# Audio tower on one core: the scan's input moves from PSUM to SBUF

## The reference, cut to what matters

```
def _ssm_layer(x, A_log, Dp, W_dbc, W_dt, b_dt):
    A = -jnp.exp(A_log)
    dbc = jnp.einsum('ble,ce->blc', x, W_dbc)
    delta, Bm, Cm = jnp.split(dbc, [DT_RANK, DT_RANK + N_STATE], axis=-1)
    delta = jax.nn.softplus(jnp.einsum('blr,er->ble', delta, W_dt) + b_dt)
    dA = jnp.exp(delta[..., None] * A)
    dBx = (delta * x)[..., None] * Bm[:, :, None, :]
    _, hs = jax.lax.associative_scan(combine, (dA, dBx), axis=1)   # h = dA * h_before + dBx
    y = jnp.einsum('blen,bln->ble', hs, Cm)
    return y + Dp * x
for i in range(NUM_LAYERS):            # 3 layers
    x = _ssm_layer(x, ...)
    if i < NUM_LAYERS - 1: x = mean of neighbouring pairs in time
h = _L0_tok_ref(x, ...)
h = h + _L0_attn_ref(_layernorm(h), ...)
h = h + _L0_ffn_ref(_layernorm(h), ...)
```

## Time and profile before

| | us |
|---|---|
| median of 3 runs | 638.44 |
| the profiled execution's own time | 639.52 |
| its span, first to last instruction | 637.8 |
| TensorE busy (matmul) | 568.4 (89%) |
| VectorE busy | 523.7 (82%) |
| ScalarE busy | 513.2 (80%) |
| GpSimd busy | 436.8 (68%) |

### The profile page before, as it was taken

One profiled execution on the slowest core, in us unless ns is written; L12 is line 12 of the kernel. 1 busy time (PEld: TensorE's weight loads), 2 busy tenths in 40 slices (PEclk: granted clock), 3 DMA queues, 4 the chain that ended last, 5 costly groups with the idle time before them and its releaser, 6 DMA issues.

```text
span 637.8 us, 22844 instructions
## 1 busy us (share of the span) xinstructions
PE 568.4 (89%) x9531; PEld 299.1 (47%) x9531; DVE 523.7 (82%) x924; ACT 513.2 (80%) x1044; POOL 436.8 (68%) x597
## 2 busy tenths in 40 slices
PE   3777678899999999999899999999999999999993
PEld 2333234545454554555454455554555544545441
DVE  5898999999979898988888988989799887653442
ACT  1335658989989999998888998999989887988780
POOL 7757899788777877876776777697785866423120
PEclk9999869999999999999999999999999999999996
DMA  3432223122121322122121222121200100000001
GB/s 78 84 80 65 57 56 73 43 59 54 40 51 26 79 50 49 36 55 52 24 61 42 61 48 60 41 65 36 65 21 20 28 20 15 20 15 10 7 13 30
DMA packets 77574, 28.51 MB, mean 45 GB/s; under 512 B 69271, under 2 KB 77463, under 8 KB 77463
## 3 DMA queue, kind: packets, MB, share of 16 engines
q1 hardware_dynamic: 71290, 25.92, 17.9%
q10 hardware_dynamic: 6173, 1.05, 0.9%
HBM read 13.25 MB, written 3.05 MB: 26 GB/s over the span
## 4 chain that ended last, share of the span: by engine, by line
PE 55%; DVE 16%; ACT 14%; POOL 6%; issue 4%; ACTq 2%; DMA 1%; SPq 1%; DVEq 0%; POOLq 0%
PE ring L1283 8%; PE ring L1362 6%; PE ring L1375 6%; PE ring L1470 5%; PE ring L1269 4%; PE ring L1441 3%; PE ring L1450 3%; PE ring L1258 2%; ACT pm L1066 2%; DVE ring L1732 2%; PE ring L1238 2%; PE ring L1421 2%; PE ring L1352 2%; DVE hidw L1860 2%; ACT hid L1116 1%
## 5 line engine op out<-in xcount | busy, mean ns | idle before, releaser
L1066 ACT ACTIVATE pm<-ring 93x744 f32<-93x744 f32 x128 | 96.3, 782 | 11.0 <-PE ring L1362 10.0
L1362 PE MATMUL ring<-q_exp,qk 32*93 32x372 f32 x512 | 56.2, 507 | 7.7 <-POOL q_exp L910 1.1
L1860 DVE TENSOR_TENSOR hidw<-hid,ring 128x744 f32<-128x744 f32 x48 | 44.3, 923 | 17.9 <-PE ring L1431 13.3
L1375 PE MATMUL ring<-pm,v 97*32 97x93 f32 x2048 | 53.5, 245 | 1.3 <-DVE base_A L1736 0.6
L1109 ACT ACTIVATE hid<-ring,b_col 128x372 f32<-128x372 f32 x96 | 49.4, 568 | 4.1 <-PE ring L1450 3.0
L1375 PEld LDWEIGHTS ring<-pm,v 97*32 97x32 f32 x2048 | 41.7, 109 | 16.0 <-ACT pm L1066 3.4
L910 POOL TENSOR_TENSOR q_exp<-qk,mask_q 128x1488 f32<-128x1488 f32 x16 | 43.0, 2687 | 8.9 <-DVE qk L1790 8.9
L1116 ACT ACTIVATE hid<-ring,b_col 128x744 f32<-128x744 f32 x48 | 42.2, 879 | 7.6 <-PE ring L1441 5.7
L893 POOL TENSOR_TENSOR base_C<-base_C,carry_C 128x744 f32<-128x744 f32 x16 | 28.4, 1777 | 27.1 <-DVE carry_C L1741 19.1
L1441 PE MATMUL ring<-hid,w 64*64 64x372 f32 x384 | 40.1, 488 | 0.6 <-ACT rows_hi_D L990 0.3
L1450 PE MATMUL ring<-nrm_f,w 64*64 64x372 f32 x384 | 39.4, 485 | 0.0
(11 more groups left out here) (366 smaller groups left out, 1757.2 us busy)
## 6 DMA issues: line engine op xcount, KB each, us to landing
xin_A<-in_x_dram SPq DMA_DIRECT2D x62, 93.0 KB
xin_B<-in_x_dram SPq DMA_DIRECT2D x62, 93.0 KB
x_A<-x_A SPq DMA_DIRECT2D x32, 93.0 KB, 3.0
x_B<-x_B SPq DMA_DIRECT2D x32, 93.0 KB, 2.7
x_C<-x_C SPq DMA_DIRECT2D x32, 93.0 KB, 2.2
out_dram<-osb SPq DMA_DIRECT2D x15, 186.0 KB
x_D<-x_D SPq DMA_DIRECT2D x32, 46.5 KB, 2.3
w<-in_L_ffn_expert_w_dram SPq DMA_DIRECT2D x6, 48.0 KB
```

What stands on the lines that cost most here:

```text
L1066: a.activation(pm[q % 2][h][0:TOUT].rearrange("m a j n -> m a (j n)"), out_of(f"att.s{q}{h}", g)[0:TOUT, :, 0:COLS], ACT.Square, bias=2.0, ...
L1362: ins = mm(o[h][0:TOUT, b, 0:COLS], qk[r:r + 32, 1, q * TOUT:(q + 1) * TOUT], q_exp[r:r + 32, q].rearrange("p j n -> p (j n)"), start=True ...
L1375: ins = mm(o[32 * j:32 * j + 32, 0, h * TOUT:h * TOUT + TOUT], rows[:, at:at + 32], pm[q % 2][h][:, b, j, :], start=(b == 0), stop=(b == 1 ...
L1860: tt(hidw[k][:], hid2[:], out_of(f"ffn.g_{k}", g)[:, :, 0:COLS], ALU.mult).then_inc(me, 1)
```

## The change

The step `vin` writes its product into the SBUF tile `carry` instead of its own PSUM banks, and the scan reads and writes that tile in place. So the wait for the `y` of the group before moves from `scan` to `vin`, and the banks of job `b` are free as soon as `vin` has ended.

```
-                for j, r in (("z", "quad"), ("b", "scan"), ("s", "based"), ("c", "carry"))}
+                for j, r in (("z", "quad"), ("b", "vin"), ("s", "based"), ("c", "carry"))}
...
                 if s == "vin":
                     need(g, f"pe {u}.b")
                     need(g, f"pool {u}.du")
-                    tt(b_made(u, g), b_made(u, g), du[u][:], ALU.mult).then_inc(me, 1)
+                    need(g, f"pool {u}.y", back=1)
+                    tt(carry[u][:], b_made(u, g), du[u][:], ALU.mult).then_inc(me, 1)
                 if s == "scan":
                     need(g, f"dve {u}.vin", f"act {u}.decay")
-                    need(g, f"pool {u}.y", back=1)
-                    v.tensor_tensor_scan(carry[u][:], dec[u][:], b_made(u, g), 0.0, ALU.mult, ALU.add).then_inc(me, 1)
+                    v.tensor_tensor_scan(carry[u][:], dec[u][:], carry[u][:], 0.0, ALU.mult, ALU.add).then_inc(me, 1)
```

The five strings of `ORDER` are new throughout. The same steps stand in them, 1000 on TensorE before and now, in another order and with other banks. A line of TensorE's and one of VectorE's:

```
-                    "att.s2:5/6,2! att.rs:6/0 ffn.h2_2:3/4! ffn.rs:4/6! att.qk:6/0 A.c:8/2! ffn.rh:4/6 B.z:9/4! B.b:9/6! "
+                    "A.c:8/2! ffn.rh:4/6 B.z:9/4! D.row:7/1! att.y2:5/2! B.b:9/6! att.s1:5/4,0! ffn.lg:4/3 ffn.g_2:3/0! "
...
-                    "A.carry:8 B.quad:9 B.vin:9 B.scan:9 ffn.route1:4 ffn.hidw2:3 B.most:9 ffn.top:4 ffn.fin:3 D.quad:7 att.hs:6 "
+                    "ffn.hn:4 A.carry:8 B.quad:9 B.vin:9 ffn.route1:4 ffn.hidw2:3 att.hs:6 ffn.top:4 A.most:9 B.scan:9 ffn.fin:3 "
```

## The result

The changed kernel takes 694.70 us (median of 3 runs, 693.01 to 695.31) against 638.44 us; the ratio is 1.0857, 95% interval 1.0832 to 1.0883. I had forecast 662.5 us, with a range of 641 to 692. The way was right, the size was not: it lost 56 us where I had forecast 24.

What follows compares the result with a forecast made beforehand. Three nearly full engines in a static order (TensorE 96%, ScalarE 92%, VectorE 89%) were taken to leave little room; 639.5 - 1.5 - 6 + 20 + 11 = 663.0, predicted as 662.5 us, range 641 to 692.

Steps and rivals of the forecast that it cites:

- Durations: In vin and the scans: vin 927 ns against 935, each scan some 18 ns shorter; 1.5 us less for both together.
- Banks freed earlier: At TensorE's waits that ended with a scan: vin frees the banks of b earlier, -6 us, bounds 0 and -12.6.
- VectorE stands still: At the scans, now with two SBUF inputs: VectorE waits for GpSimd instructions, 34 to 48 us, taken as 40.
- GpSimd is held: Where GpSimd's next instruction falls in a scan, it waits for the scan's rest: 44 us with the present positions.
- The rows of `rest` and the rests: Rows of a small two-SBUF-input VectorE instruction: it stands until GpSimd's is over, 0.14 us covered, losing 2 of 5 gapless boundaries.
- How much of this reaches the end: Over the whole kernel: half of VectorE's delay, 20 us, and a quarter of GpSimd's, 11 us, lengthen the run.
- Rival 1: At the scans: they don't take GpSimd's port, so only earlier banks and durations count; 631 us, chance 0.12.
- rival 2: At the scans: stalls come but fall into VectorE's and GpSimd's idle time; 642.5 us, chance 0.11.
- Rival 3: At gapless GpSimd boundaries: scans lose more often than 2 in 5, VectorE becomes the bound; 701 us, chance 0.07.
- Some 92%: TensorE's busy share from 120 to 500 us, forecast to fall from 96% to about 92%.
- The scans' means of 2.2 to 2.4 us: Sign in the changed profile: groups of scans would have a mean of 2.2 to 2.4 us, well over 1700 ns.
- TensorE's clock: In the steady stretch: the granted clock was expected to stay full; under full would add an uncounted cost.

Runs made afterwards that it cites:

- e2: The changed kernel with its orders and banks, each scan replaced by a reduction of the same length reading one SBUF tensor, recurrence left out: 633.7 us, ratio 0.9899.
- e3: The kernel before with old orders and the new step, each scan replaced by a same-length reduction reading one SBUF tensor: 639.9 us, ratio 1.0012.
- e1: The kernel before with its own orders and banks, only the step changed (vin writes the carry tile, scan works there): 695.2 us, ratio 1.0885.
- e10: As e6, with each VectorE stall half as long (31 of them, 18.2 us): 649.2 us, ratio 1.0137.
- e6: e2 with the changed kernel's 43 VectorE stalls (37.8 us) put back as idle reductions ahead of the scans: 669.9 us, ratio 1.0462.
- e7: e2 with the changed kernel's 51 GpSimd stalls (57.4 us) put back as idle additions: 664.0 us, ratio 1.0373.

## Why the prediction was right in its direction and wrong in its size

- *Durations.* `vin` 927 ns as forecast. A scan that nothing holds takes 1689 to 1708 ns, 1678 to 1704 before: the 18 ns that I took off each don't show. Together some 0.5 us, where I had 1.5.
- *Banks freed earlier,* -6 us: e2 has 0.9899 of before, 6.4 us, but that my number meets it is in part luck. I had it from the waits that ended with a scan (half of 12.6 us), and with the old order the earlier release gave nothing (e3). Only with the new order does it bring something, and I had not told the two apart.
- *VectorE stands still,* 34 to 48 us, I took 40: measured 37.8. *GpSimd is held,* 44 us: measured 57.4, so I was too small by 13. That is worth 3 us at my share. The new order is not why: with the old one (e1) GpSimd's busy time rose by 58.9 us, from 436.8 to 495.7. I had read it off the positions of the kernel before. 31 of the 51 holds were of 1.27 to 1.41 us: a scan that gets in where one GpSimd instruction ends meets the next one at its start and holds it for nearly the whole scan, which the old positions don't show.
- *The rows of `rest` and the rests.* Of VectorE's 34 us for the instructions under way, the trace gives 31 when 0.14 us are taken off each, as I said I did; that is worth under 2 us. And where I wrote that `rest` at 524.32 us starts before a GpSimd addition, it starts inside another GpSimd instruction (the row below, which I had left out). So it was passed over at three gapless boundaries there, 3 of 6 and not 2 of 5. The scans' 9 of 29 came out lower than either.

```profile
524.12 0.33 POOL L919 TENSOR_SCALAR oh<-logit 93x48 f32<-93x48 f32 x1
```

- *How much of this reaches the end.* Here the prediction failed. "I let half of VectorE's delay through: 20 us", and a quarter of GpSimd's, 11 us: 31 us. Measured, 62.7 us reached the end. VectorE's share alone is 96 to 97% (e10, e6), GpSimd's alone 59% (e7), both together 66%. With 66% of my own 40 + 44 the sum would have been 639.5 - 7.5 + 55 = 687, 686 in the median's terms. (The sum as I had it gives 661.9 in those terms; I wrote 662.5.)

Why the shares were wrong: I read 40 us of VectorE's idle time as room for delays. It isn't. With 37 us of work put ahead of the scans (e6), VectorE was busy 380.0 of 420 us, 90%, and 377.7 in e2; over the whole run it was idle for 110.6 us in e6 and 110.7 in e2, so its idle time did not shrink. TensorE's busy time in the 420 us fell instead, from 405 to 385. The waits of that stretch say how: those of TensorE's weight loads that ended with VectorE sum to 46 us in e2 and 68 in e6, and ScalarE's that ended with TensorE to 26 and 55. The longest of those of TensorE that ended with VectorE in e6 (us in total, times, longest) stands behind the 5.40 us of work put ahead of one scan of unit C:

```profile
PEld ring L1397 <- DVE attT L1808: 5.6, 1, 5.6
```

A delay of one engine turns into a wait of the others a few jobs on. The chain of waits had hinted at it: it changes engine all the time. From it I took the engine's share of the chain (19%) as a lower end, and that said little about VectorE: the chain shows one path, and others through VectorE must have been nearly as long, which no view shows directly; in e6 VectorE has 29% of the chain, 17% in e2.

Rival 1 (scans don't take the port) and rival 2 (idle time takes the stalls in) are out. Rival 3 (VectorE starves) named a mechanism that is there, 9 passed boundaries and stalls of 4.5 and 5.4 us, but it is not what made the size: VectorE stood for 37.8 us, within my bounds. "Some 92%" for TensorE was wrong: 88%. The scans' means of 2.2 to 2.4 us, which I had named as a sign, hold for A and C alone; B's is 1.88, and D's 1.90 where 0.92 is its own length. TensorE's clock, which I took to stay full, fell to a mean of 0.97 from 120 to 540 us; the fall at 184 us comes right behind an idle time. TensorE's busy time is 13.0 us over e2's (578.8 and 565.8) for the same matmuls. How much of the 63 us that is wasn't measured by itself; it comes along with the holds too (e6: 576.8 us busy, mean clock 0.952), so the delays bring it, and it is part of the shares above.

By the rule that the prediction quoted from the Trainium skill (SBUF — State Buffer, Who interferes with whom), the trace agrees, for scans as well: they stand while GpSimd reads, and GpSimd stands while they run. At a gapless boundary between two GpSimd instructions the waiting scan got in 20 times, and GpSimd's next instruction went ahead of it 9 times.

## What to carry to other kernels

Before an operand of a VectorE instruction is moved from PSUM to SBUF, count its SBUF inputs: if the move makes them two and GpSimd is busy beside it, the overlap of the two engines (here 76 of 96 us of scans) turns into standing time on one or the other, which a row of a small instruction of that kind can show beforehand by its longest case. In a static order over several engines that are each about 90% busy, as here, charge a delay on the engine that the others wait for at its full length, not at half, and one on an engine that is 76% busy at more than half: idle shares were no slack. And try such a step with the old order first (e1), since a new order can hide how dear the step is, and a later reader can't tell the two apart.

## What the runs showed of the hardware that I had not expected

- The standing doesn't end with the GpSimd instruction under way: one scan stood for 5.4 us beyond its 1.70, over four GpSimd instructions. A gap of some 0.08 us between two of them, where GpSimd waits for its own result, was enough to let VectorE in each of the 12 times that a standing scan met one.
- A scan, which takes 2.1 ns an element, holds GpSimd too: instructions of 0.50 us took 1.78.
- Where its second input comes from makes no difference beyond a few ns to a scan that nobody disturbs: 1678 to 1704 ns with PSUM, 1689 to 1708 with SBUF.
